# Two-slot steps, a wide inverse, one residual buffer and moved x loads in a fused group-norm attention kernel

## What is computed

```python
h = group_norm(x, 32 groups) * scale + bias          # statistics over all tokens of a batch
q, k, v = split(h @ qkv_w + qkv_b)                   # each 1024 x 512
q, k, v = (a.reshape(batch * 8, 1024, 64) for a in (q, k, v))   # no transpose of heads
weight = softmax((q / 64 ** 0.25) @ (k / 64 ** 0.25).T)
out = x + (weight @ v).reshape(batch, 1024, 512) @ proj_w + proj_b
```

## Time and profile before

| what | value |
|---|---|
| median of 3 runs | 3845.33 us (3835.63 to 3846.1) |
| the profiled execution, its own time | 3851.28 us |
| its span, first to last instruction | 3848.4 us |
| mean granted TensorE clock | 0.994 of 2.4 GHz |
| chain that ended last | PE 84%, SPq 4%, ACT 4%, issue 3%, DVE 2%, DMA 1% |
| DMA | mean 169 GB/s, packets on the main queue 69.7% of 16 engines' span |

### The profile page before, as it was taken

How to read it: one execution, slowest core, us unless ns; L and a number is a source line. 1 busy time by engine, 2 the same in 40 slices (tenths; PEclk the granted TensorE clock), 3 DMA queues, 4 the chain that set the end, 5 groups by cost and what they waited for, 6 DMA issues and landing times.

```text
span 3848.4 us, 77013 instructions
## 1 busy us (share of the span) xinstructions
PE 3663.7 (95%) x24128; PEld 2805.1 (73%) x24128; DVE 2780.5 (72%) x3473; ACT 2435.3 (63%) x4753; POOL 1829.1 (48%) x3018
## 2 busy tenths in 40 slices
PE   6999999999999999999999999999999999999998
PEld 5777777777777777777777777777777777777775
DVE  4777777777777777777777777776776777777776
ACT  6666666566665766666666666566665666665763
POOL 4455454444454544445445445444454544454551
PEclk9999999999999999999999999999999999999999
DMA  3767677777676767777777676766767677677766
GB/s 116 183 164 179 166 173 170 167 178 168 165 173 166 181 161 173 168 170 180 166 168 167 167 184 158 172 166 166 180 163 172 164 169 181 158 178 168 170 161 166
DMA packets 255911, 648.82 MB, mean 169 GB/s; under 512 B 73872, under 2 KB 73872, under 8 KB 255376
## 3 DMA queue, kind: packets, MB, share of 16 engines
q1 hardware_dynamic: 254224, 638.35, 69.7%
q10 hardware_dynamic: 1152, 4.19, 0.3%
HBM read 71.84 MB, written 33.55 MB: 27 GB/s over the span
## 4 chain that ended last, share of the span: by engine, by line
PE 84%; SPq 4%; ACT 4%; issue 3%; DVE 2%; DMA 1%; POOL 0%; ACTq 0%; POOLq 0%; DVEq 0%
PE pv_ps L412 23%; PE s_ps L379 13%; PE s_ps L381 11%; PE c_ps L452 5%; PE c_ps L453 5%; PE c_ps L454 5%; SPq L343 4%; PE pv_ps L392 4%; ACT staged L526 3%; PE c_ps L437 3%; PE c_ps L435 3%; PE c_ps L436 3%; PE c_ps L463 2%; PE c_ps L465 2%; PE c_ps L464 2%
## 5 line engine op out<-in xcount | busy, mean ns | idle before, releaser
L638 DVE TENSOR_REDUCE neg_max<-s_ps 128x1 f32<-128x1024 f32 x1024 | 1242.2, 1213 | 940.8 <-PE s_ps L381 940.4
L512 ACT ACTIVATE probs<-s_ps,neg_max 128x1024 f32<-128x1024 f32 x1024 | 1143.8, 1117 | 1217.3 <-DVE neg_max L638 1206.2
L619 DVE STREAM_TRANSPOSE turned<-probs 128x1024 f32<-128x1024 f32 x1024 | 1263.8, 1234 | 3.3 <-DMA probs_t<-turned 2.5
L412 PE MATMUL pv_ps<-probs_t,v 128*64 128x256 f32 x8192 | 994.1, 385 | 10.0 <-DMA probs_t<-turned 10.0
L526 ACT ACTIVATE staged<-c_ps,qk_bias 64x256 f32<-64x256 f32 x2048 | 956.8, 467 | 30.9 <-PE c_ps L454 10.1
L761 POOL CAST attn_hi<-attn 128x256 fp32r<-128x256 f32 x256 | 102.0, 398 | 1448.7 <-DVE attn L632 1200.4
L412 PEld LDWEIGHTS pv_ps<-probs_t,v 128*64 128x64 f32 x8192 | 562.4, 138 | 308.3 <-issue 81.0
L452 PE MATMUL c_ps<-h_hi,w_hi 128*128 128x256 f32 x2048 | 582.6, 284 | 64.1 <-ACT staged L526 57.7
L453 PE MATMUL c_ps<-h_lo,w_hi 128*128 128x256 f32 x2048 | 578.0, 282 | 0.0
L454 PE MATMUL c_ps<-h_hi,w_lo 128*128 128x256 f32 x2048 | 577.2, 282 | 0.0
L452 PEld LDWEIGHTS c_ps<-h_hi,w_hi 128*128 128x128 f32 x2048 | 388.1, 189 | 100.8 <-ACT staged L526 74.5
(11 more groups left out here) (75 smaller groups left out, 5790.4 us busy)
## 6 DMA issues: line engine op xcount, KB each, us to landing
probs_t<-turned SPq DMA_DIRECT2D x4096, 128.0 KB, 2.3
x_res<-in_x SPq DMA_DIRECT2D x128, 256.0 KB, 2.7
result<-x_res SPq DMA_DIRECT2D x128, 256.0 KB, 2.6
x_next<-in_x SPq DMA_DIRECT2D x120, 256.0 KB, 2.8
probs_t<-in_L_conv_qkv_w ACTq DMA_DIRECT2D x4, 768.0 KB, 8.7
turned<-in_x SPq DMA_DIRECT2D x4, 512.0 KB, 12.8
probs_t<-in_L_conv_proj_w ACTq DMA_DIRECT2D x4, 256.0 KB, 13.8
v_bias<-in_L_conv_qkv_b SPq DMA_DIRECT2D x1, 256.0 KB, 16.9
```

The costliest lines, as they stand in the source:

```text
L412: last = nc.tensor.matmul(pv_ps[side][CH * par:CH * (par + 1), 0, :], v_sb[:, ring_of(i, parity), CH * chunk:CH * (chunk + 1)], p_t[:, par ...
L512: nc.scalar.activation(probs[k % 2][:, :], s_ps[k % 2][:, :], ACT.Exp, bias=neg_max[:, k % 4:k % 4 + 1], accum_out=row_sum[:, (k // HALF) ...
L619: nc.vector.transpose(dst, probs[(k - 1) % 2][:, :].rearrange("p (k b j) -> p k b j", k=CHUNKS, b=QUADS)).then_inc(probs_turned, 1)
L638: nc.vector.tensor_reduce(neg_max[:, k % 4:k % 4 + 1], s_ps[k % 2][:, :], AX.X, ALU.max, negate=True).then_inc(max_ready, 1)
```

## The change

- Slots are taken in steps of two on PE, ACT and DVE. In even slots PE runs the scores of k and k + 1; its large and small units and the attends stay in their slots.
- ACT runs, per step: take_inverse (k % 4 = 0), the exponentials of k and k + 1, `norm_x` for both parts (k % 16 = 0, now of the next pair), then staging and x copy of k, then of k + 1.
- DVE runs, per step: the maxima of k and k + 1, scale_attn (k % 4 = 0), the v unit of the step before (k % 16 = 0), the turn of k, v or proj of slot k + 1, the turn of k + 1 (turns are no longer a slot behind), the inverse (k % 4 = 2), statistics.
- The reciprocal writes each inverse 64 times, 128 x 256; PE spreads it with two 128 x 128 transposes in place of four 128 x 64 matmuls. Row sums have a ring of 4.
- `STAT_SLOTS` and the slots that follow from them move; all of the statistics slots are odd, and the two group slots even.
- `MOVE_LAG` is 4; SP stores before it moves, and loads x and residual at k % 4 = 3 (x for the batch's first tile at k = 0). The residual ring has one buffer in place of two.
- POOL's `split_attn` is at k % 4 = 1, behind `split_qk` of the slot before; `add_bias` is at m = 9 and m = 1.
- `dynamic_dma_scratch_size` is 1024 in place of 512.

```diff
-STAT_SLOTS = [1, 10, 14, 17, 21, 26, 36, 38]
-AGGREGATE_SLOT = 40
-GROUP_MEAN_SLOT = 41
-GROUP_VAR_SLOT = 43
-AFFINE_SLOT = 44
-NORM_SLOT = 14
+STAT_SLOTS = [1, 5, 9, 13, 21, 29, 37, 41]
+AGGREGATE_SLOT = 42
+GROUP_MEAN_SLOT = 44
+GROUP_VAR_SLOT = 46
+AFFINE_SLOT = 47
-MOVE_LAG = 5
+MOVE_LAG = 4
+INVERT_LAG = 6
...
-        x_res = sb("x_res", [P, XRING, C])
+        x_res = sb("x_res", [P, C])
...
-        inv_sum = sb("inv_sum", [P, 2, HALF])
+        inv_wide = sb("inv_wide", [P, HALF * CH])
...
             def slot(b, k):
-                if k % HALF == MOVE_LAG % HALF:
-                    move_half(b, k)
-                if k % 16 == 0:
-                    load_residual(b, 2 * (k // 16) - 1)
-                if k % 16 == 8:
-                    load_residual(b, 2 * (k // 16))
+                if k == 0:
+                    load_x_tile(b, 0)
                 if k % 16 == 4:
                     store(b, 2 * (k // 16) - 2)
                 if k % 16 == 12:
                     store(b, 2 * (k // 16) - 1)
-                if k == 0:
-                    load_x_tile(b, 0)
-                if k in STAT_SLOTS[:-1]:
-                    load_x_tile(b, STAT_SLOTS.index(k) + 1)
+                if k % HALF == MOVE_LAG % HALF:
+                    move_half(b, k)
+                if k % 16 == 7:
+                    load_residual(b, 2 * (k // 16) - 1)
+                if k % 16 == 15:
+                    load_residual(b, 2 * (k // 16))
+                if k - 2 in STAT_SLOTS[:-1]:
+                    load_x_tile(b, STAT_SLOTS.index(k - 2) + 1)
...
-                for i in range(HALF):
-                    par, u = i % 2, i // 2
-                    last = nc.tensor.matmul(pv_ps[side][CH * par:CH * (par + 1), 1, u * P:(u + 1) * P],
-                                            inv_sum[:, side, i:i + 1].broadcast_to([P, CH]), ident[:, :],
-                                            start=True, stop=True)
+                for u in range(2):
+                    last = nc.tensor.transpose(pv_ps[side][:, 1, u * P:(u + 1) * P], inv_wide[:, u * P:(u + 1) * P],
+                                               ident[:, :])
...
-                if within(s, N_SLOTS):
+                if k % 2 == 0 and within(s, N_SLOTS):
                     scores(b, k)
+                    scores(b, k + 1)
                 large(b, k)
                 small(b, k)
...
+            def step(b, k):
...
                 if within(s, N_SLOTS):
                     softmax_exp(b, k)
+                    softmax_exp(b, k + 1)
+                if k % 16 == 0 and within(made_pair(b, k), N_PAIRS):
+                    norm_x(b, k, 0)
+                    norm_x(b, k, 1)
+                for slot in (k, k + 1):
+                    kind, n, _ = large_unit(slot)
+                    if kind == "qk" and within(made_pair(b, slot), N_PAIRS):
+                        stage_qk(b, slot, n)
+                    if small_unit(slot)[0] == "stats" and within(b + 1, BATCHES):
+                        copy_x(b, slot)
...
-                at_least(dve, inv_full, half - 1)
-                nc.vector.reciprocal(inv_sum[:, n % 2, :], row_sum[:, n % 2, :]).then_inc(inv_ready, 1)
+                at_least(dve, inv_full, half)
+                sums = row_sum[:, n % 4, :].rearrange("p (s a) -> p s a", a=1).broadcast_to([P, HALF, CH])
+                nc.vector.reciprocal(inv_wide[:, :].rearrange("p (s c) -> p s c", s=HALF), sums).then_inc(inv_ready, 1)
...
+            def step(b, k):
+                s = SPB * b + k
+                if within(s, N_SLOTS):
+                    largest(b, k)
+                    largest(b, k + 1)
+                if k % HALF == EVAC_LAG % HALF and within(s - EVAC_LAG, N_SLOTS):
+                    scale_attn(b, k)
+                if k % 16 == 0:
+                    if k > 0:
+                        take_v(b, k - 1)
+                    elif not before_start(b):
+                        take_v(b - 1, SPB - 1)
+                if within(s, N_SLOTS):
+                    turn(b, k)
+                kind, _, part = large_unit(k + 1)
+                if kind == "v" and large_unit(k + 1)[1] == 1:
+                    take_v(b, k + 1)
+                if kind == "proj":
+                    take_proj(b, k + 1)
+                if within(s, N_SLOTS):
+                    turn(b, k + 1)
+                if k % HALF == INVERT_LAG % HALF and within(s - INVERT_LAG, N_SLOTS):
+                    invert(b, k)
                 statistics(b, k)
...
-                if k % HALF == EVAC_LAG % HALF:
-                    split_attn(b, k // 4 - EVAC_LAG // HALF)
+                if k % HALF == (EVAC_LAG + 1) % HALF:
+                    split_attn(b, (k - 1) // HALF - EVAC_LAG // HALF)
...
-                if m == 15:
-                    add_bias(b, 2 * pair)
+                if m == 9:
+                    add_bias(b, 2 * pair - 1)
+                if m == 1:
+                    add_bias(b, 2 * pair - 2)
```

More of the change, by code:

```diff
@@ L176, in attention_block @@
         pool_chain = sem("pool_chain")
-        x_loaded = [sem(f"x_loaded{i}") for i in range(XRING)]
-        stored = [sem(f"stored{i}") for i in range(XRING)]
+        x_loaded = sem("x_loaded")
+        stored = sem("stored")
         x_start_loaded = [sem(f"x_start_loaded{i}") for i in range(PPB)]
@@ L288, in batches, with in_steps @@
                 slot(BATCHES, k)
+        def in_steps(step):
+            return lambda b, k: step(b, k) if k % 2 == 0 else None
         def at_least_aside(engine, sem, count):
@@ L356, in slot @@
                     store(b, 2 * (k // 16) - 1)
-                if k == 0:
-                    load_x_tile(b, 0)
-                if k in STAT_SLOTS[:-1]:
-                    load_x_tile(b, STAT_SLOTS.index(k) + 1)
+                if k % HALF == MOVE_LAG % HALF:
[6 more added lines that the diff above has]
+                    load_x_tile(b, STAT_SLOTS.index(k - 2) + 1)
             batches(sp, slot)
-            for ring in range(XRING):
-                sp.wait_ge(stored[ring], 16 * N_BLOCKS // XRING)
+            sp.wait_ge(stored, 16 * N_BLOCKS)
         @block.tensor
@@ L572, in slot @@
                     softmax_exp(b, k)
[L573 to L582, removed]
+                    softmax_exp(b, k + 1)
[8 more added lines that the diff above has]
+                        copy_x(b, slot)
+                    if before_start(b) and slot in STAT_SLOTS[1::2]:
+                        round_qkv_weights(STAT_SLOTS.index(slot) // 2)
+                    if before_start(b) and slot == STAT_SLOTS[-1]:
+                        round_proj_weights()
             for t in range(KT):
@@ L587, in _ @@
                 act.dma_start(pw_stage[t], proj_w[t * P:(t + 1) * P, :]).then_inc(pw_loaded, 16)
-            batches(act, slot)
+            batches(act, in_steps(step))
         @block.vector
@@ L610, in turn @@
             def turn(b, k):
-                t = SPB * b + k - 1
-                n, i = (k - 1) // HALF, (k - 1) % HALF
+                t = SPB * b + k
+                n, i = k // HALF, k % HALF
                 half = 2 * BLOCKS * b + n
@@ L632, in scale_attn, with largest, take_v @@
                 nc.vector.tensor_tensor(attn[:, :], pv_ps[side][:, 0, :], attn[:, :], ALU.mult).then_inc(attn_scaled, 1)
-            def slot(b, k):
+            def largest(b, k):
+                dve.wait_ge(scores_full, SPB * b + k + 1)
+                nc.vector.tensor_reduce(neg_max[:, k % 4:k % 4 + 1], s_ps[k % 2][:, :], AX.X, ALU.max,
+                                        negate=True).then_inc(max_ready, 1)
+            def take_v(b, k):
+                n, g = large_unit(k)[1], v_pair(b, k)
+                if not within(g, N_PAIRS):
+                    return
+                parity = (k // 16) % 2 if n else (k // 16 + 1) % 2
+                dve.wait_ge(v_full, 2 * g + n + 1)
+                if n == 0 and within(g - 1, N_PAIRS):
+                    dve.wait_ge(pv_done, 4 * (g - 1) + 2)
+                if n == 1 and within(g - 2, N_PAIRS):
+                    dve.wait_ge(pv_done, 4 * (g - 1))
+                nc.vector.tensor_tensor(v_sb[:, ring_of(n, parity), :], bank(k, LARGE)[:, :], v_bias[:, :],
+                                        ALU.add).then_inc(v_ready, 1)
@@ L635, in slot, with take_proj @@
+            def take_proj(b, k):
+                n, h = large_unit(k)[1], proj_block(b, k)
+                if not within(h, N_BLOCKS):
+                    return
+                dve.wait_ge(proj_full, h + 1)
+                dve.wait_ge(residual_ready, h + 1)
+                nc.vector.tensor_tensor(x_res[:, :], bank(k, LARGE)[:, :], x_res[:, :], ALU.add).then_inc(out_ready, 1)
+            def step(b, k):
                 s = SPB * b + k
                 if within(s, N_SLOTS):
-                    dve.wait_ge(scores_full, s + 1)
@@ L638, in slot @@
[L638 to L641, removed]
+                    largest(b, k)
+                    largest(b, k + 1)
```

(4 more changed lines are left out.)

33 lines of the change are left out of this document (12 added, 21 removed).

## The result

The changed kernel takes **4321.7 us** (median of four runs, 4318.4 to 4329.4) against 3842.0 before (four runs, 3835.6 to 3846.1): a ratio of **1.125 [1.123, 1.128]**. It is slower, as forecast, but by 480 us where 185 were forecast, and it lies above the upper end of the range, 4140.

The account below looks back on a forecast made before the run. PE bounds the kernel, by its in-order work plus waits, chiefly for c_ps banks. Per batch 22.9 us added less 10.4 gone, net +12.5, came to +185 together: 4036 profiled, 4031 us as median; range 3930 to 4140.

Parts of the forecast that it names:

- second stand for issue: Top of PE's loop: only the existing issue wait, 32.0 us, once per turn, was expected, and to stay.
- spread by two transposes: PE's spread of the inverses: two transposes replace the narrow records, gaining 0.22 us a half, 3.5 a batch.
- c_ps rule: On PE's c_ps banks: a tenant waits until the tenant two before it is taken out; no size itself.
- the seven waits: Transposes of x behind qk units, slots 5 to 41: PE loses 1.90 us seven times, 13.3 a batch.
- the wide reciprocal: DVE's reciprocal over 256 columns: taken as 0.39 us, like the same-width scaling row, lying in DVE's slack.
- The order on ACT: On ACT, exponentials k and k+1 both ahead of staging; by itself this costs 0.
- Slot 45: Its qk unit waits for slot 44's staging, after the group mean and late DVE: 4.0 us lost a batch.
- Slot 48: Its v unit waits for DVE to take out slot 46's, because of the group variance: 2.6 us a batch.
- Proj for attn_lo: Proj waits for POOL's later split_attn after steps 24 and 56: 1.5 us twice, 3.0 a batch; about 30 waits.
- x_next: PE's wait for the next x load, 27.0 us over 15 batches, goes: 1.8 and 0.15 us a batch.
- Rival A: The reciprocal on 256 columns is dear, 1.7 us, making DVE late: some 7 a batch, +105, 4135; chance 0.09.
- PE busy near 91%: Sign expected in the profile of the changed kernel: PE's busy share, against 95% before.

Follow-up runs that it names:

- a_copy: Changed kernel with a four-column reciprocal and a DVE copy that widens it to 128x256; 4158.5 us, 1.081 of the kernel before.
- b_copy_stats_pad: Kernel before with narrow reciprocal, copy, two transposes, later inverse, one residual buffer, other statistics slots, eight unread matmuls ahead of the loop; 3728.6 us, 0.969.
- a_copy_order: a_copy with unit k staged on ACT between exponentials k and k+1 instead of after both; 4025.7 us, 1.047 of the kernel before.
- a_fill: Changed kernel with 14 unread matmuls ahead of each of the seven waiting groups of x transposes per batch; 4197.2 us, 1.092 of the kernel before.
- a_copy_fill: a_copy with unread matmuls ahead of every new wait of PE (transposes, qk in slot 45, v in slot 48, proj); 4043.7 us, 1.051 of the kernel before.

## Why the prediction was right in its waits and wrong in its size

The spans differ by 471.5 us: PE stands 340.7 longer (525.4 for 184.7) and is busy 130.8 longer. The rows above divide this:

| part | predicted | measured | from |
|---|---|---|---|
| new waits of PE less those gone | +240 | +232 | four rows of after, 417.1, less 103.3, less the next line |
| the same, lengthened by the reciprocal | 0 | +82 | after less a_copy |
| second stand for issue | 0 | +33 | 64.8 less 32.0 |
| spread by two transposes | -56 | -56 | PE busy, before and b_copy_stats_pad; 42 to 50 by the other pairs |
| lower clock | 0 | +187 | PE busy 3794.5 less 3607.3 |
| sum | +185 | +478 | the spans say +471.5 |

Only the rows of waits can miss the total, and they do by 6 us; the last two lines add up to the 130.8 of busy time whatever is put on the spread. The clock's line has two other readings. 441 less 46 us at the lower level, where work takes twice as long, is 197, an upper bound, since PE also stood in that time. By the granted clock PE is busy for 378 of the 440 us, and for 44 of 48 before: half the difference is 167. So the clock is worth some 170 to 190.

**The c_ps rule and the seven waits: right.** 105 waits as counted, and in a_copy 1.75 of idle each, where 1.90 less 0.15 of tail were written; in after itself they are 2.36 each, by the wide reciprocal. The order on ACT, "by itself 0", is what makes nearly half of these waits: a_copy_order has 86 us less of them.

**Slot 45: right.** 4.0 was written; in a_copy it is 4.04 in fourteen of the fifteen batches that have it and 3.97 in the first; the other waits of its row, short ones but for two of 3.1, stand in the first 90 us and in the last batch. In after it is 4.86, since DVE is later still. **Slot 48: right**, 39.5 over 16 is 2.5 for 2.6. **Proj for attn_lo: nearly**, 34 times for 30, 1.2 each for 1.5. x_next no longer appears among PE's main waits.

**The wide reciprocal: wrong, and one of the two failed steps.** The prediction took 0.39, "the row of the same width", between that and 1.7. It measured 1.71. The upper bound, from the aggregate's rate, hit this value, but nothing ties the two instructions together: that is luck. The page VectorE: DVE Perf Modes of the Trainium skill, section "First, the fixed hardware budget", has a repeat count of 8 for the divide, by which the prediction estimated 2.1; the row agrees with it in kind (1.71 us for 256 columns are 6.7 ns each, against 1.1 for the copy) and is below it in size. Choosing by width was no argument, since the scaling row multiplies and the disputed row divides. Nor is the aggregate "the dearest DVE row per element", as written: the narrow reciprocal is, with 158 ns for 4 columns. Rival A had this price, its mechanism (DVE late in front of the waits) and a cost of 105; its waits were 82, and with the clock behind them 163. It got a chance of 0.09.

**The clock: wrong, and the larger failure.** No term of the sum and no rival had it. The profile of before had a clock of 0.994, and I carried the full-speed durations into a kernel to which I had just given over 300 us of new standing. The runs show some 187 us of slower work in place of this 0. a_fill and a_copy_fill show that the standing is what lowers it: work put into it makes the kernel faster. "PE busy near 91%" wasn't even the forecast's own sum: 3663.7 - 56 of 4033 are 89.5%. It came out at 87.8%, because PE stood longer; the slower clock, which makes the same work longer, held the share up.

**The second stand at the loop's top: wrong, small.** I wrote that the one stand "stays"; a second one joined it. It costs 33 us, and 10 to 15 more behind it. Eight matmuls ahead of the loop remove it, in each of three kernels, so it doesn't hang on what the change computes. That the place of the loop's code decides it is the likeliest reading, since the matmuls shift the first scores by at most 1.3 us and the stand is gone from all 13 turns; but no run holds the time and moves the code alone, and what makes the stand is open.

The prediction's own tests told the first failure at once, the reciprocal's row over 1 us. They had none for the second: PE's share hides it, and what tells it is the granted clock and a busy time that rose with fewer instructions.

## What to carry to other kernels

Price a wait of PE twice: the time it stands, and the slower clock of the matmuls behind it; here 340 us more of standing came with some 187 us of slower work. Not each wait costs the same in this: in after those of 2.5 and 4.9 us were followed by it nearly each time, those of 2.4 50 times in 105, and those of 1.7 in a_copy 14 times in 105. Price an elementwise instruction by its operation, not by its width: here the wide divide cost 163 us more than a narrow one and a copy. And before a kernel's order is judged, look for a second stand at the top of the loop, since eight matmuls ahead of the loop made it go here.

## What the runs showed that was not expected

- A reciprocal of 128x256 lasts 1710 ns, of 128x4 135 to 158; a copy of 128x256 lasts 294.
- 1456 matmuls that nobody reads made the kernel 125 us faster, some 45 of it because the second stand for issue went.
- The stand for issue at the loop's top comes once or twice per turn (27 to 43 us each for 13 of them), and eight matmuls that run once, ahead of the loop, decide it: 44, 50 and 60 us in three pairs of kernels.
